# A six-layer transformer stage: q's and k's parts stored one by one and fetched in one transfer, the last head group normalised by itself, and a new written-out order

## Chip, cores and metric

The kernel runs on one core of a Trainium2 chip. The metric is the device time of one execution in microseconds (us), lower is better. TensorE (PE) does the matrix products, VectorE (DVE), ScalarE (ACT) and GpSimd (POOL) the rest, and SyncE (SP) issues every DMA of the stage that is changed.

## What is computed

The whole model adds eight blocks to a residual stream of 2 x 512 tokens of width 128. The change lies in the third, a transformer of six layers with 16 heads of width 8 and a context of 77 tokens. Its reference, cut to what matters:

```python
for i in range(NL):                                   # NL = 6
    xn = _adaln(x, noise_emb, n1_w[i], n1_b[i])       # layer norm, modulated
    q, k, v = jnp.split(xn @ qkv_w[i].T, 3, axis=-1)
    q, k = _rope(q), _rope(k)                         # B = 2, L = 512, H = 16, HD = 8
    x = x + _attn(q, k, v, src_mask).reshape(B, L, D) @ so_w[i].T
    xn = _adaln(x, noise_emb, n2_w[i], n2_b[i])
    q = _rope(xn @ cq_w[i].T); k = _rope(context @ ck_w[i].T); v = context @ cv_w[i].T
    x = x + _attn(q, k, v, ctx_mask).reshape(B, L, D) @ co_w[i].T
    xn = _adaln(x, noise_emb, n3_w[i], n3_b[i])
    x = x + gelu(xn @ f1_w[i].T + f1_b[i]) @ f2_w[i].T + f2_b[i]
```

`_attn` is a softmax over masked scores. All arithmetic is float32 in the reference.

## The kernel before

**Tiling.** A batch (one of two, `c`) has 512 tokens, four tiles of 128. Heads are taken in four groups of four (`HG` = 4). A step `a` = 2 x layer + batch is one self-attention, twelve in all; `rest(r)` is everything around it: for `r` from 2 on the cross attention and the feed-forward net that follow step `r - 2`, and for `r` below 12 the first layer norm and the q, k and v projections that precede step `r`.

**Three bfloat16 parts.** q and k are float32 values kept as three bfloat16 parts (high, middle, last). A score is a product over 48 rows of parts: six blocks of 8 rows, the block numbers of q and k paired by `Q_PARTS = (0, 0, 1, 0, 2, 1)` and `K_PARTS = (0, 1, 0, 2, 0, 1)`. The tiles `qS`, `kS` and `cS` (k of the context) hold these 48 rows, then a mask row (48) and rows for the maximum (96, 97). The projections leave q and k as 128 partitions (head x 8 + dim) x 512 tokens; the parts are made in `part3` (inside `room`) by a chain that alternates between POOL and ACT: `join` (POOL L1466), high part (ACT L1224), `rest_part` (POOL L1470), middle part (ACT L1228), `last_part` (POOL L1474). Getting them from head-major partitions into dim-major rows goes through DRAM: one store of all three parts (SP, L1549), then six transfers of 8 partitions each (`spread`, L1556), each `d h t` out of `(h d) t` in runs of 512 tokens.

**One self-attention** has two passes. The first (`maxima`, letter `m`) is 64 score products (PE L975), each reduced to a row maximum (DVE L1307) out of two PSUM banks; after each group of 16 the maxima are turned (PE L957), copied (ACT L1177) and sent into `qS` by four small DMAs (SP L1537). The second (`attend`, letter `a`) is 64 score products again (PE L1013), each with an exponential (ACT L1195), 16 times four products with V (PE L997, `weigh`), a copy of each head group's output (ACT L1186, `keep_out`), and then the normalisation: V has columns of ones, so that the outputs hold the softmax sums; POOL adds the four groups' outputs (L1447, L1443), DVE takes one reciprocal of 128 x 512 (L1321), spreads the wanted row with a shuffle per group (L1328) and multiplies groups 0 and 2 (L1333), POOL multiplies groups 1 and 3 (L1452). Then PE projects group by group (L1025, four products of 128 columns for a group, each recorded as two matmuls) and DVE adds the result to the stream `z` (L1336). The cross attention has the same scheme for all four groups: reductions L1388, reciprocal L1399, multiplications L1411 and L1506, projection L1122. The letter `r` is a piece of `rest`.

**The order of the work** on each engine is fixed by hand: each engine has generators `m`, `a` and `r`, and `weave` takes one piece of a stream per letter of the strings in `TURNS`. Before, a string has a first part, a part for a layer that is repeated, and a last part. An engine goes through its queue in order and waits at semaphores.

## Time and profile before

| | |
|---|---|
| runs | 5213.22, 5220.8, 5223.22 us, median 5220.8 |
| the profiled execution | 5205.5 us, of which its span 5203.7 |
| mean granted TensorE clock | 0.879 of 2.4 GHz over the span |
| transformer stage (2060 to 3823 us of the span) | 54 us of preparation, then 1709 us |
| busy shares over the span | PE 84%, DVE 65%, ACT 44%, POOL 10% |

Times are read from the start of the span. "Busy" counts instructions that compute; an engine's idle time before an instruction is put down to what released it. The granted clock is given as a share of full speed: 1.00 is 2.4 GHz, 0.50 is 1.2 GHz.

### The profile page before, as it was taken

How to read it: one execution, taken by the hardware profiler on the slowest of the kernel's cores; microseconds unless marked ns; L12 is line 12 of the kernel's file. 1: busy time of each engine (PE TensorE's matmuls, PEld its weight loads, DVE VectorE, ACT ScalarE, POOL GpSimd, SP SyncE). 2: the span in 40 equal slices, each digit the busy share in tenths (PEclk: the TensorE clock that was granted, in tenths of full speed). 3: DMA queues.
4: the chain of work that ended last, by engine and by line, in shares of the span. 5: the costliest groups of instructions: out<-in, count | busy, mean ns of one | idle time of the engine just before them, and what ended most of it. 6: DMA issues, size and time to landing. Idle time of an engine off the chain costs nothing. (4 is left out here: it accounts for less than half of the span.)

```text
span 5203.7 us, 88732 instructions
## 1 busy us (share of the span) xinstructions
PE 4381.7 (84%) x25098; PEld 2768.5 (53%) x25446; DVE 3406.6 (65%) x17506; ACT 2302.0 (44%) x7385; POOL 504.0 (10%) x420
## 2 busy tenths in 40 slices
PE   8999999999999987587787878778733697997979
PEld 6888888888888865223333333333322453333456
DVE  7888888888888876455555555555434594433535
ACT  4555555555555543263545454545422122332313
POOL 0000000000000001111221212222101001222000
PEclk9999999999999988697878787878765698998769
DMA  0000000000000001302222222221100010000001
GB/s 27 2 2 2 2 2 2 2 2 2 2 2 2 2 8 43 51 14 34 38 35 38 34 38 34 37 35 30 18 5 3 14 35 24 9 8 10 19 1 37
DMA packets 89492, 91.41 MB, mean 18 GB/s; under 512 B 21311, under 2 KB 84442, under 8 KB 88811
## 3 DMA queue, kind: packets, MB, share of 16 engines
q1 hardware_dynamic: 89067, 86.46, 8.6%
q8 instruction: 179, 2.93, 0.2%
q14 instruction: 246, 2.02, 0.1%
HBM read 70.22 MB, written 15.39 MB: 16 GB/s over the span
## 5 line engine op out<-in xcount | busy, mean ns | idle before, releaser
L287 DVE CUSTOM_DVE_ANT_0 I-219junk<-I-215encw,I-218expo,I-227rec 128x77 f32<-128x77 f32 x3072 | 941.1, 356 | 5.8
L1307 DVE TENSOR_REDUCE I-41381nmax<-ps 128x1 f32<-128x512 f32 x768 | 498.3, 686 | 235.7 <-PE ps L975 225.6
L1195 ACT ACTIVATE I-41384prob<-ps 128x512 f32<-128x512 f32 x768 | 428.6, 594 | 247.5 <-remote 135.4
L265 ACT ACTIVATE I-217tanh_s<-ps 128x77 f32<-128x77 f32 x1024 | 242.4, 237 | 593.9 <-PE ps L245 593.9
L245 PE MATMUL ps<-I-212hist,I-49small 128*128 128x77 f32 x2048 | 456.5, 304 | 40.6 <-DVE I-212hist L323 40.4
L245 PEld LDWEIGHTS ps<-I-212hist,I-49small 128*128 128x128 f32 x2048 | 304.9, 188 | 296.8 <-DVE I-212hist L323 296.7
L251 PE MATMUL ps<-I-217tanh_s,I-49small 128*128 128x77 f32 x2048 | 454.7, 304 | 0.0
L975 PE MATMUL ps<-I-41375kS,I-41374qS 96*128 96x512 bf16 x768 | 347.4, 479 | 111.4 <-DMA I-41374qS<-parts 53.3
L252 PE MATMUL ps<-I-212hist,I-49small 128*128 128x128 f32 x2048 | 440.0, 297 | 0.0
L247 PE MATMUL ps<-I-212hist,I-216uh_h 128*128 128x128 f32 x2048 | 439.8, 296 | 0.0
L273 ACT ACTIVATE I-223hh<-I-229gate_t,I-228pre,I-222rh 128x1 f32<-128x1 f32 x1024 | 395.5, 386 | 84.6
L248 PE MATMUL ps<-I-212hist,I-49small 128*128 128x128 f32 x2048 | 394.1, 273 | 0.0
L237 PE MATMUL ps<-I-49small 128*128 128x77 f32 x2048 | 350.9, 253 | 1.8 <-PEq L68 1.8
L323 DVE SCALAR_TENSOR_TENSOR I-212hist<-I-223hh,I-225zc,I-226zh 128x1 f32<-128x1 f32 x1024 | 224.7, 219 | 190.1 <-ACT I-223hh L273 190.1
L251 PEld LDWEIGHTS ps<-I-217tanh_s,I-49small 128*128 128x128 f32 x2048 | 304.7, 188 | 27.7
L237 PEld LDWEIGHTS ps<-I-49small 128*128 128x128 f32 x2048 | 311.1, 192 | 2.0 <-issue 2.0
L252 PEld LDWEIGHTS ps<-I-212hist,I-49small 128*128 128x128 f32 x2048 | 311.3, 192 | 0.0
L247 PEld LDWEIGHTS ps<-I-212hist,I-216uh_h 128*128 128x128 f32 x2048 | 311.2, 192 | 0.0
L248 PEld LDWEIGHTS ps<-I-212hist,I-49small 128*128 128x128 f32 x2048 | 311.0, 192 | 0.0
L1013 PE MATMUL ps<-I-41374qS,I-41375kS 128*128 128x512 bf16 x677 | 252.4, 402 | 58.0 <-ACT I-41384prob L1195 46.8
L115 POOL TENSOR_TENSOR I-59rstd<-I-58var,I-60mhalf 128x4 f32<-128x4 f32 x34 | 34.7, 1021 | 2741.9 <-DVE I-58var L99 2741.9
L257 PE MATMUL ps<-I-213zeros 128*128 128x512 bf16 x768 | 291.3, 379 | 0.0
(494 smaller groups left out, 7980.0 us busy)
## 6 DMA issues: line engine op xcount, KB each, us to landing
I-41374qS<-parts SPq DMA_DIRECT2D x144, 128.0 KB
parts<-I-41393room SPq DMA_DIRECT2D x36, 384.0 KB, 2.5
I-41375kS<-parts SPq DMA_DIRECT2D x72, 128.0 KB
I-49small<-in_layers SPq DMA_DIRECT2D x6, 768.0 KB, 19.2
I-41374qS<-I-41383mrow SPq DMA_DIRECT2D x192, 2.0 KB
I-41374qS<-I-41390crow SPq DMA_DIRECT2D x192, 2.0 KB
I-41393room<-in_own SPq DMA_DIRECT2D x5, 387.0 KB, 4.0
I-41368wk<-in_own SPq DMA_DIRECT2D x6, 320.0 KB, 12.8
```

The lines of the kernel that those rows point to most:

```text
L237: e.matmul(att[b][:, 0:S], w_e, encT[:, b * S:(b + 1) * S], start=True, stop=False)
L245: e.matmul(att[b][:, 0:S], w_h, now.to_broadcast([P, S]), start=False, stop=True).then_inc(s.att_ps, 1)
L247: e.matmul(row[:, H * wide:(H + 1) * wide], uh_h[:], now, start=True, stop=True, skip_group_check=True)
L248: e.matmul(row[:, R * wide:(R + 1) * wide], uh[:, R * P:(R + 1) * P], now, start=True, stop=True, skip_group_check=True)
L251: e.matmul(sco[b][:, 0:S], v_rep, tanh_s[:, b, :], start=True, stop=True).then_inc(s.scores, 1)
L252: e.matmul(row[:, Z * wide:(Z + 1) * wide], uh[:, Z * P:(Z + 1) * P], now, start=True, stop=True, skip_group_check=True).then_inc(s.u_ps, 1)
L257: e.matmul(k.ps[:, 7, :], zeros[:, 0:P], zeros[:], start=True, stop=True)
L273: e.activation(hh[:, b:b + 1], gate_t[:, b, R:R + 1], ACT.Tanh, scale=rh[:, b:b + 1], bias=pre[:, b, H:H + 1]).then_inc(s.hh_done, 1)
L287: return e.tensor_tensor_reduce(junk[:, 2 * g + b, :], encw[:, g, b, :], expo[:, b, :], inv[:, b:b + 1], rec[:, b, g:g + 1], ALU.mult, ALU ...
L975: e.matmul(k.ps[:, b, :], qS[0:ROWS_QK, 4 * m + j, c * T + i * P:c * T + (i + 1) * P], kS[0:ROWS_QK, 4 * m + j, c * T:(c + 1) * T], start= ...
L1195: e.activation(prob[:, tau % 2, j, :], k.ps[:, b, :], ACT.Exp, scale=scale).then_inc(free[b], 1)
L1307: e.tensor_reduce(nmax[:, U % HG, i, j:j + 1], k.ps[:, use[0], :], AX.X, ALU.max, negate=True).then_inc(free[use[0]], 1)
```

## The change

1. **Stores and spread.** The columns of the q, k, cross-q and cross-k weights are copied into dim-major order on POOL (`by_dim`, into new tiles `wk_d` and `wq_d`; `wq` is now a single buffer), so the projections leave q and k with partition dim x 16 + head. The cosine and sine tables are loaded again in that order by eight DMAs in the preparation. The DRAM tensor `parts` has six places instead of three. Each part is stored by itself as soon as it is made, into all of its places (three, two and one); one transfer then moves all 48 rows, in which the heads and tokens of a row lie one behind the other (16 KB). `qS`, `kS` and `cS` have the batch ahead of the head for that. The mask row takes four DMAs instead of two, and the memset of `cS` writes bfloat16 instead of float32.
2. **Normalisation.** POOL adds groups 0 to 2 only; DVE takes their reciprocal, and one more reciprocal for group 3 when that is there. Group 3 is multiplied on DVE instead of POOL. The same in the cross attention. Fewer columns of V are set to zero.
3. **Order.** All strings of `TURNS` are new and written out to the end, no part repeated. On SP, a layer's cross stores come ahead of the weights' loads.

```diff
-        parts_dram = nc.dram_tensor("parts", (4, 3, P, T), BF16).ap()
+        parts_dram = nc.dram_tensor("parts", (4, 6, P, T), BF16).ap()
...
+        Q_SPOTS = (slice(0, 3), slice(4, 6), slice(3, 4))
+        K_SPOTS = (slice(2, 5), slice(1, 6, 4), slice(0, 1))
...
-                    def store(name, n, m):
+                    def store(name, n, m, which, spots):
                         spot = SPOT[name]
-                        e.wait_ge(s.last, job[r, name])
-                        if times(r, name) > 1:
-                            e.wait_ge(jsent[spot], 96 * (times(r, name) - 1))
-                        e.dma_start(parts_dram[spot, :, :, 0:m].rearrange("r p t -> p r t"),
-                                    part3[:, n, :, 0:m]).then_inc(jstored[spot], 16)
-
-                    def spread(name, m, dst, order):
+                        e.wait_ge((s.jhigh, s.middle, s.last)[which], job[r, name])
+                        if which == 0 and times(r, name) > 1:
+                            e.wait_ge(jsent[spot], 16 * (times(r, name) - 1))
+                        dst = parts_dram[spot, spots, :, 0:m].rearrange("r p t -> p r t")
+                        e.dma_start(dst, part3[:, n, which, 0:m].unsqueeze(1).to_broadcast(dst.shape)).then_inc(jstored[spot], 16)
+
+                    def spread(name, m, dst):
                         spot = SPOT[name]
-                        e.wait_ge(jstored[spot], 16 * times(r, name))
-                        for row, which in enumerate(order):
-                            e.dma_start(dst[8 * row:8 * row + 8, :, c * m:(c + 1) * m],
-                                        parts_dram[spot, which, :, 0:m].rearrange("(h d) t -> d h t", d=8)).then_inc(jsent[spot], 16)
+                        e.wait_ge(jstored[spot], 48 * times(r, name))
+                        e.dma_start(dst[0:ROW_MASK, c, :, :],
+                                    parts_dram[spot, :, :, 0:m].rearrange("r (d h) t -> (r d) h t", h=NH)).then_inc(jsent[spot], 16)
+
+                    def deliver(name, n, m, dst, places):
+                        for which, spots in enumerate(places):
+                            store(name, n, m, which, spots)
+                            yield
+                        spread(name, m, dst)
+                        yield
...
+                    def by_dim(dst, src, ready):
+                        e.tensor_copy(dst[:, 0:512].rearrange("p (n d h) -> p n d h", n=4, d=8),
+                                      src[:, 0:512].rearrange("p (n h d) -> p n d h", n=4, d=8)).then_inc(ready, 1)
...
-                    e.wait_ge(s.pooled, 3 * (a + 1))
-                    e.reciprocal(inv[:], inv[:]).then_inc(s.inv, 1)
-                    yield
                     for n in range(HG):
                         U = HG * a + n
-                        e.wait_ge(s.inv, a + 1)
+                        if n == 0:
+                            e.wait_ge(s.pooled, 2 * (a + 1))
+                            e.reciprocal(inv[:], inv[:]).then_inc(s.inv, 1)
+                            yield
+                        if n == HG - 1:
+                            e.wait_ge(*done(values(a, n)))
+                            e.wait_ge(s.wide, U)
+                            e.reciprocal(inv[:], o[:, n, :]).then_inc(s.inv, 1)
+                        e.wait_ge(s.inv, 2 * a + 1 + n // (HG - 1))
                         if U >= 2:
                             e.wait_ge(s.normed, U - 1)
                         e.stream_shuffle(wide[:, n % 2, :], inv[:], [8 + n] * 32).then_inc(s.wide, 1)
-                        if n % 2 == 0:
+                        if n != 1:
```

Written out by name from the strings, this is PE's queue around the end of step 5 (S: scores of the second pass, W: `weigh`, O: output projection of a group, M: maxima of step 6, R6 and R7: pieces of `rest`; "ln2" the turn of a layer norm, "qx" q's projection, "kx" the context's k, "cv" the context's values, "sx", "tx", "txs" projections of k and q, "v" of the values):

```text
before  S5.14.0-1 W13 R6.txs R6.v0 S5.14.2-3 S5.15.0 R6.v1 R6.v2 S5.15.1 W14 S5.15.2-3 R6.v3 R7.kx W15 O0 O1 O2 O3 R7.ln2 R7.qx R7.cv M6.0.0 ...
after   R6.txs ... R6.v3 R7.kx S5.12.0 ... S5.14.2-3 S5.15.0-1 W14 S5.15.2-3 W15 O0 O1 O2 O3 M6.0.0-3 R7.ln2 M6.0.4-5 R7.qx R7.cv M6.0.6 ...
```

At the very start PE's queue before has the projections of `R0` and `R1` (16 pieces) and then the maxima of step 0; after it has those of `R0` (8 pieces), then 29 pieces of step 0's maxima and their turn up to M0.1.4 with the two passes and `R1` mixed from there on. Around step 2, txs of `R2` is 10 pieces ahead of M2.0.0 before and 31 pieces after. DVE's queue around the end of step 5 is, before, `R6.tturn recip N0 N1 N2 N3 add R7.ln2`, and after the same names in the same order, with the second reciprocal inside N3; in the cross attention of `R6` it is, after, `M5.2.7 recip N0 N1 M5.2.8 N2 N3 M5.2.9`.

## Rows read from the trace of the kernel before

**Rows 1.** Windows by stage: time, busy of each engine (instructions), clock, DMA share, GB/s

```profile
2060.00:2114.00 54.00, 15.52 (x72) 15.43 (x72) 25.29 (x12) 0.14 (x1) 19.12 (x27) 0.50 0.17 51
2114.00:3823.00 1709.00, 1322.44 (x6509) 534.73 (x6600) 925.29 (x1908) 815.38 (x1560) 328.48 (x300) 0.81 0.20 33
```

**Rows 2.** Groups by line, 2060 to 3900 us: busy, mean ns, idle before, releasers

```profile
L1307 DVE TENSOR_REDUCE I-41381nmax<-ps 128x1 f32<-128x512 f32 x768 | 498.3, 686 | 235.7 <-PE ps L975 225.6
...
L975 PE MATMUL ps<-I-41375kS,I-41374qS 96*128 96x512 bf16 x768 | 347.4, 479 | 111.4 <-DMA I-41374qS<-parts 53.3 <-DVE I-41381nmax L1307 43.0 <-ACT I-41383mrow L1177 0.2
L1013 PE MATMUL ps<-I-41374qS,I-41375kS 128*128 128x512 bf16 x677 | 252.4, 402 | 58.0 <-ACT I-41384prob L1195 46.8 <-issue 5.2
...
L1025 PE MATMUL ps<-I-41369wso,I-41385o 128*128 128x128 f32 x384 | 73.9, 370 | 72.6 <-DVE I-41385o L1333 72.5
...
L1086 PE MATMUL ps<-I-41376cS,I-41374qS 96*128 96x77 bf16 x768 | 61.0, 236 | 32.8 <-DMA I-41374qS<-parts 30.1 <-issue 0.7 <-DVE I-41388cmax L1388 0.2
...
L1321 DVE RECIPROCAL I-41387inv<-I-41387inv 128x512 f32<-128x512 f32 x12 | 40.2, 3353 | 154.5 <-POOL I-41387inv L1443 154.5
L1399 DVE RECIPROCAL I-41392cinv<-I-41392cinv 128x512 f32<-128x512 f32 x12 | 40.2, 3350 | 39.5 <-POOL I-41392cinv L1496 39.5
```

**Rows 3.** PE in order of time: start, us [idle before and its releaser]

```profile
2162.07 1.03 PE L975 MATMUL ps<-I-41375kS,I-41374qS 96*128 96x512 bf16 x2 [12.97 <-DMA I-41374qS<-parts]
...
2395.78 1.03 PE L975 MATMUL ps<-I-41375kS,I-41374qS 96*128 96x512 bf16 x2 [19.12 <-DMA I-41374qS<-parts]
...
2788.13 5.42 PE L1025 MATMUL ps<-I-41369wso,I-41385o 128*128 128x128 f32 x24 [7.09 <-DVE I-41385o L1333]
...
3722.38 2.84 PE L1025 MATMUL ps<-I-41369wso,I-41385o 128*128 128x128 f32 x24
...
3794.54 6.57 PE L1122 MATMUL ps<-I-49small,I-41393room 128*128 128x128 f32 x32 [7.06 <-DVE I-41393room L1411]
```

**Rows 4.** ACT and DVE in order of time: the work between the two

```profile
2781.11 0.60 ACT L1186 ACTIVATE I-41385o<-ps 128x512 f32<-128x512 f32 x1 [1.19 <-PE ps L997]
...
2786.47 0.72 DVE L1328 STREAM_SHUFFLE I-41386wide<-I-41387inv 128x512 f32<-128x512 f32 x1
2787.29 0.69 DVE L1333 TENSOR_TENSOR I-41385o<-I-41385o,I-41386wide 128x512 f32<-128x512 f32 x1
```

**Rows 5.** Windows around one such wait, columns as in rows 1

```profile
2784.00:2786.00 2.00, 0.00 (x0) 0.00 (x0) 2.00 (x1) 0.00 (x0) 0.00 (x0) 0.50 1.03 141
...
2812.00:2822.00 10.00, 8.36 (x18) 1.94 (x19) 8.65 (x15) 1.57 (x3) 1.15 (x1) 0.50 0.21 56
2840.00:2848.00 8.00, 7.33 (x64) 2.86 (x63) 6.03 (x16) 6.28 (x14) 0.00 (x0) 1.00 0.02 5
```

**Rows 6.** The way of the last cross q through DRAM, in order of time

```profile
3742.43 1.15 POOL L1474 TENSOR_TENSOR I-41393room<-I-41393room 128x512 bf16<-128x512 f32 x1 [0.74 <-ACT I-41393room L1228]
3743.61 0.38 SPq L1549 DMA_DIRECT2D parts<-I-41393room  x1
3746.16 2.10 SPq L1556 DMA_DIRECT2D I-41374qS<-parts  x6
...
3759.40 2.23 PE L1086 MATMUL ps<-I-41376cS,I-41374qS 96*128 96x77 bf16 x24 [21.84 <-DMA I-41374qS<-parts]
```

**Rows 7.** Windows with a spread alone, and with the first loads of the program

```profile
3746.00:3758.00 12.00, 0.00 (x0) 0.00 (x0) 0.00 (x0) 0.00 (x0) 0.00 (x0) 0.50 0.49 65
...
4.00:6.00 2.00, 0.00 (x0) 0.00 (x0) 0.00 (x0) 0.00 (x0) 0.00 (x0) 1.00 1.08 430
```

**Rows 8.** POOL's end of q's parts for step 0

```profile
2132.75 1.15 POOL L1474 TENSOR_TENSOR I-41393room<-I-41393room 128x512 bf16<-128x512 f32 x1 [0.74 <-ACT I-41393room L1228]
```

**Rows 9.** The preparation, DVE and SP in order of time

```profile
2068.68 1.08 DVE L882 MEMSET I-41376cS<- 128x1232 f32 x1 [0.20 <-issue]
...
2087.41 2.11 DVE L885 MEMSET I-41376cS<- 2x2464 bf16 x1 [0.46 <-issue]
...
2091.03 0.58 SPq L845 DMA_DIRECT2D I-41376cS<-I-41393room  x1
```

More of the change, by code:

```diff
@@ L786, in rest_order, with transformer @@
     return out
-def transformer(nc, k, small, z, ctxT, own_dram, layers, masks, rows, sel_dram):
+def transformer(nc, k, small, z, ctxT, own_dram, layers, masks, rows, small_dram):
     with ExitStack() as ctx:
@@ L843, in _ @@
                 e.wait_ge(s.filled, 4)
-                for dst, row in ((kS, maskrow[:, 0:B * T]), (cS, maskrow[:, B * T:B * (T + S)])):
-                    e.dma_start(dst[ROW_MASK:ROW_MASK + 1, :, :],
-                                row.unsqueeze(1).to_broadcast([1, NH, row.shape[1]])).then_inc(s.sent, 16)
-                e.wait_ge(s.sent, 16 * 2)
+                for c in range(B):
+                    for dst, at, m in ((kS, c * T, T), (cS, B * T + c * S, S)):
+                        e.dma_start(dst[ROW_MASK:ROW_MASK + 1, c, :, :],
+                                    maskrow[:, at:at + m].unsqueeze(1).to_broadcast([1, NH, m])).then_inc(s.sent, 16)
+                e.wait_ge(s.sent, 16 * 2 * B)
                 e.dma_start(mods[0], own_dram[0][:, 0:774]).then_inc(s.mods, 16)
-                e.wait_ge(s.own, 16 * 2)
+                at = offsets(SMALL)[0]["cos"][0]
+                for d in range(8):
+                    e.dma_start(small[16 * d:16 * d + 16, at:at + 2 * T], small_dram[d:P:8, at:at + 2 * T]).then_inc(s.own, 16)
+                e.wait_ge(s.own, 16 * 10)
             @block.gpsimd
@@ L858, in _ @@
                     for g in range(HG):
-                        for n in range(HG):
-                            if n != g:
+                        for n in range(HG - 1):
+                            if n != g and g < HG - 1:
                                 e.memset(dst[:, :, 4 * g:4 * g + 4, 8 + n:9 + n], 0.0).then_inc(s.ones, 1)
@@ L983, in attend @@
                     l, c = divmod(a, B)
-                    tok = slice(c * T, (c + 1) * T)
                     def weigh(t):
@@ L1162, in rest @@
                             b = open_bank(e, use)
-                            e.matmul(k.ps[:, b, 0:P], mine[:, i * P:(i + 1) * P], K(4), start=True, stop=True).then_inc(full[b], 1)
+                            e.matmul(k.ps[:, b, 0:P], mine[:, i * P:(i + 1) * P], wk[:, 512:640], start=True, stop=True).then_inc(full[b], 1)
                             yield
@@ L1222, in high_part @@
                             last = jobs[job[r, name] - 3]
-                            e.wait_ge(jstored[SPOT[last[1]]], 16 * times(*last))
+                            e.wait_ge(jstored[SPOT[last[1]]], 48 * times(*last))
                         e.activation(part3[:, n, 0, 0:m], flat[:, n, 0:m], ACT.Copy).then_inc(s.jhigh, 1)
@@ L1597, in rest @@
                     if r < NA:
-                        store("k", 0, T)
-                        yield
-                        store("q", 1, T)
-                        yield
-                        spread("k", T, kS, K_PARTS)
-                        yield
-                        spread("q", T, qS, Q_PARTS)
-                        yield
+                        yield from deliver("k", 0, T, kS, K_SPOTS)
+                        yield from deliver("q", 1, T, qS, Q_SPOTS)
                 weave(TURNS["sync"], m=all_of(maxima), r=all_rest(rest))
@@ L2343, in model @@
         layer_norm(nc, k, x, nT, keep=z)
-        transformer(nc, k, small, z, g_("ctxT"), A["own"], A["layers"], (A["mask1"], A["mask2"]), A["l1f2b"], A["sel"])
+        transformer(nc, k, small, z, g_("ctxT"), A["own"], A["layers"], (A["mask1"], A["mask2"]), A["l1f2b"], A["small"])
         add_stream(nc, x, z)
```

250 lines of the change are left out of this document (145 added, 105 removed).

## The prediction

> **What bounds the kernel now.** I read the windows by stage first. The transformer stage takes 54 us of preparation and 1709 us of work; in the latter PE is busy 1322 us (77%), DVE 925 (54%), ACT 815, POOL 328, at a mean granted clock of 0.81 [rows 1]. So PE's queue is the longest, and 387 us of it are gaps. The groups by line name them [rows 2]: PE stands 72.5 us at the output projection (L1025) for the normalised groups, 53.3 us at the first maxima (L975) and 30.1 us at the first cross maxima (L1086) for a DMA of parts, 46.8 us at the scores for an exponential, 43.0 us at the maxima for DVE's reductions. In order of time these are few and long: 12.97 us ahead of step 0, 19.12 us ahead of step 2, 7.09 us at the end of a step, 7.06 us in the last cross attention [rows 3]; at the very end 21.84 us for the last cross q [rows 6]. The remaining waits for parts, 53.3 - 12.97 - 19.12 = 21.2 us in nine and 30.1 - 21.84 = 8.3 us in four, are 2 us each. Since PE stands there with nothing else to do, a us taken from such a wait is a us of the kernel, as long as no other wait takes its place.
>
> **The way through DRAM.** The last cross q shows it alone [rows 6]: the last part is done at 3743.6, the store is issued at once, the spread at 3746.16 (2.55 us later) and PE starts at 3759.4, 13.2 us after that. The six transfers move 786 KB at 65 GB/s with 0.49 to 0.57 of 16 engines busy, which is 12 us [rows 7]. That is eight partitions at a time in runs of 1 KB. The same queue moved the program's first loads, 128 partitions with long rows, at 430 GB/s [rows 7]. The new spread has 48 partitions and rows of 16 KB. Its moving time lies between 786 KB / 430 = 1.8 us and the old 12 us; I take 4, nearer the fast end since both the run length and the number of partitions go the way of that row, plus the 2 us that a small transfer needs here anyway (2.55 for the store): 6 us from issue to landing for 13.2. The store of the last part alone has a third of the bytes, and the others are issued under POOL's and ACT's chain: 2.2 us for 2.55. One trip falls from 15.8 to 8.2 us; bounds 6 and 16.
>
> The Trainium skill (DMA: Bandwidth & Descriptors, "Why a DMA increments its semaphore by 16 and not by 1") says that a transfer is split over the largest number of engines up to 16 that divides the slowest dimension of both sides: eight for the old transfers, sixteen for the new, and the half-busy engines agree with that. Its page SBUF — State Buffer ("Door 1") puts partitions 0 to 47 on 8 of 16 ports of 435 GB/s together; by that the new spread moves at 218 GB/s at most, 3.6 us.
>
> **The terms**, summed against the profiled execution's own 5205.5 us.
>
> *Start, -18.* q's parts of step 0 are ready at 2133.9 [rows 8], but PE starts its maxima only at 2162.1 [rows 3]: k's and q's spreads share the queue, then weights and the next batch's stores come in. With 8.2 us and k's ahead of it, 2144 is due after the preparation is 2.3 us later: the memset of `cS` in bfloat16 costs 2.11 for 1.08 by the row of the same number of columns, and two more mask DMAs at 0.6 us each lie on SP ahead of the modulation's load [rows 9]. By that step 0 starts 18 us earlier. R1's pieces now lie between its maxima; PE is paced by DVE's 0.62 us there and has room, and the second pass starts 8 maxima sooner, so I set these against each other. Bounds -8 and -25. The reload of the sine tables (8 DMAs) and the first POOL copy lie under the modulation's matmuls and under DVE's first norm; uncovered they'd cost about 3 and 1.3 us.
>
> *Step 2, -17.* PE's 19.12 us [rows 3] end with q's landing. Before, q's last projection (txs) is 10 pieces ahead of the maxima, now 31; PE's queue has 2616 pieces, 0.65 us each over 1709 us [rows 1], so 20 us instead of 6.5. The parts take 6 us from the projection (3737.6, where PE's 21.84 us begin, to 3743.6 [rows 6]), k's begin about 2 us ahead of q's, and two spreads of 4 us follow: 6 + 2 + 8 + 2 = 18 at most. About 2 stay.
>
> *End of a step, -49.* Between PE's last weighing (2781.0) and its next matmul lie the copy of group 3 (0.60), POOL's sum, the reciprocal (3.35), a shuffle (0.72) and a multiplication (0.69): 7.09 us [rows 2 to 4]. Groups 0 to 2 no longer wait: group 2 is complete sixteen exponentials earlier, and DVE is idle there (154.5 us of idleness ahead of L1321 in 12 steps [rows 2]). Group 3 needs 0.60 + 3.35 + 0.72 + 0.69 and some 0.35 of hand-overs, 5.7 us, during which PE projects three groups, 2.84 us at full clock [rows 3], up to 3.7. What stays is 2.0 to 2.9; I take 2.4 of a mean 6.6 in eleven places: -46, and -3 for the twelfth and for POOL's multiplications, which are off the way. What is queued behind DVE's new wait in N3 is only the addition to z, which waits for PE anyway.
>
> *Small waits for parts, -20.* Nine and four waits, 29.5 us in all, with 7 us taken from each trip; a third is kept, since 18 us against 20 is a narrow margin at each step.
>
> *The clock, -20.* After the 7 us wait the granted clock is 0.50, still 0.50 from 2812 to 2822, and 1.00 from 2840 on [rows 5]. The first 24 matmuls of L1025 took 5.42 us there and 2.84 at 3722, where no long wait came first [rows 3]: 2.6 us, and about 1 more for the projections behind it; the DVE-paced maxima lose nothing. 3.6 x 10 = 36; the shorter waits still lower it at times, so I take about half. Bounds 0 and -36.
>
> *The end, -12.* 7.6 from the last trip and 4.6 from the last cross projection's 7.06.
>
> *Costs, +10.* DVE gets 24 reciprocals and 24 multiplications more, 24 x (3.35 + 0.69) = 97 us. The twelve of the self-attention fall into its idleness. The twelve of the cross attention are among the maxima, with only 39.5 us idle ahead of the old one [rows 2]; PE's next maxima must wait out 3.35 us or find other work. Bounds 0 and +40; a quarter, since PE's order has scores and weighings there. POOL's 13 copies of 128 x 512 (about 1.2 us, as its other operations of that size [rows 6]) replace 24 additions and fall between norms, where it is idle; uncovered 16 us. Zeroed columns are fewer. The smaller number of issues on SP (4 for 7) is worth nothing to PE.
>
> *The order, -10.* 90 us of PE's waits (exponentials and reductions, [rows 2]) can be moved only by the order of the queues, for either sign. R6's projections leave the last quarter of a step, which ACT paces, for its middle. Bounds -40 and +25.
>
> Sum: -18 - 17 - 49 - 20 - 20 - 12 + 10 - 10 = -136. The profiled execution would be 5069.5; against the median of the runs, which lies 15 us above it, 5085.
>
> **The rivals.**
> *The spread is only half as fast* (12%), 8 us of moving for 4. For it: each old transfer, too, filled single partitions, and 16 engines at the old 8 GB/s each (65 over 8) give 6. Then k's and q's last landing is 26 us behind txs for PE's 20: 6 us at each of ten steps instead of the third kept, start -12, end -8, half the clock: 5130.
> *DVE becomes the limit* (12%). If the 97 us delay the reductions by 55 beyond my 10, 5140. For it: PE already waits 43.0 us for reductions and is paced by them in the first groups of a step; against it: DVE 54% busy, becoming 60%.
> *The order recovers more* (20%): the clock stays up and the waits for exponentials shrink, 6 us for each of ten steps, 5025.
> *Slower* (5%): the spread stays at 65 GB/s. For it: one transfer is issued where six were, and if it is not split over more engines, nothing makes it faster. k and q then move for 24 us in a row, and q lands 6 + 2 + 24 + 2 = 34 us behind txs where PE arrives after 20; some of that PE's order absorbs at a lower pace, I take 11 left at each of ten steps. Start -4, step 2 -10, step ends -49, waits for parts +85, end -5, clock 0, costs +10, order -10: +17, 5238. It decides from a moving time of about 11 us on; with four engines it would be +200 and more. Against it: the row of 430 GB/s, and loads later in the program whose DRAM side is one contiguous piece.
> *No change* (2%): new waits cancel the gain.
>
> **How the numbers follow.** 49% for the forecast (5060 to 5115), 12, 12, 20, 5 and 2% for the others. 5020 to 5160 holds the forecast, both weak gains and half of the strong one: a little over 8 in 10. Within 0.2% (10 us, what a measurement of this kernel can tell) lies 3%; slower 5%; faster 92%.
>
> **What would show it.** The wait at L1025 for DVE: 20 to 30 us in all instead of 72.5, now at the fourth group. L975 and L1086 for parts under 20 together, for 83. Spread from issue to PE's start about 6 us at the end, windows above 150 GB/s. First maxima at 2144. Mean clock of the stage 0.85 or more. Idle PE for reductions above 60 us would show DVE's rival. The prediction is wrong if the steps, 133.5 us apart between 2788 and 3722 (seven steps, [rows 3]), stay above 130, whatever the start gives.

## The result and the profile after

The changed kernel takes 5090.43 us (median of 5089.45, 5089.49, 5091.37 and 5112.34), the one before 5219.66 (four runs, 5213.22 to 5223.22): a ratio of 0.9764, 95% interval 0.9736 to 0.9792. The forecast was 5085. The profiled execution is the one of 5112.34 us; its transformer stage ends (L121) at 3709.9 against 3829.9, 119.9 us earlier. Behind the stage the two kernels are the same, and there this execution lost 27 us again. The windows of the last stretch show that, first of after, then of before (columns as in rows 1):

```profile
4500.00:5110.00 610.00, 537.30 (x2198) 304.95 (x2196) 248.05 (x547) 164.60 (x290) 48.28 (x24) 0.79 0.05 15
```

```profile
4620.00:5203.00 583.00, 511.19 (x2196) 290.27 (x2195) 248.28 (x547) 164.01 (x289) 48.26 (x24) 0.83 0.05 16
```

The same matmuls (2198 and 2196 records) take 26 us more of PE at a granted clock of 0.79 instead of 0.83. The other three runs of after are some 22 us shorter, at a mean clock of 0.889 to 0.891 for 0.886; where in them the time was saved no trace shows. Such swings are in several kernels here (one gave 5067.5 to 5112.3 us, with a mean clock of 0.894 to 0.884), so below I read small effects at the end of the transformer stage, and whole kernels by ratios.

The windows by stage, of after [compare rows 1]; as there, the second window ends 6.9 us before the stage's end:

```profile
2060.00:2116.00 56.00, 15.52 (x72) 15.44 (x72) 26.32 (x12) 0.00 (x0) 18.16 (x15) 0.50 0.19 59
2116.00:3703.00 1587.00, 1284.00 (x6600) 526.10 (x6600) 1018.67 (x1956) 817.26 (x1560) 282.81 (x270) 0.84 0.20 45
```

The work is 122 us shorter than in [rows 1]; PE is busy 81% of it, DVE 64%, the clock is 0.84 for 0.81. (Before, 91 of PE's records are missing, all at L1013, so that some 30 us of its busy time there may stand as idle.) The groups by line, 2060 to 3731 us [compare rows 2]:

```profile
L1005 PE MATMUL ps<-I-41377kS,I-41376qS 96*128 96x512 bf16 x768 | 331.5, 460 | 131.2 <-DVE I-41383nmax L1336 67.7 <-DMA I-41376qS<-parts 50.8 <-ACT I-55xh L1239 2.9
L1042 PE MATMUL ps<-I-41376qS,I-41377kS 128*128 128x512 bf16 x768 | 281.1, 408 | 53.2 <-ACT I-41386prob L1224 45.1 <-DMA I-41376qS<-I-41385mrow 3.6
...
L1115 PE MATMUL ps<-I-41378cS,I-41376qS 96*128 96x77 bf16 x768 | 67.1, 247 | 16.7 <-DMA I-41376qS<-parts 15.6 <-DVE I-41390cmax L1422 0.3
...
L1054 PE MATMUL ps<-I-41369wso,I-41387o 128*128 128x128 f32 x384 | 50.3, 283 | 24.6 <-DVE I-41387o L1367 21.1 <-issue 3.5
...
L1358 DVE RECIPROCAL I-41389inv<-I-41387o 128x512 f32<-128x512 f32 x12 | 40.2, 3353 | 28.3 <-ACT I-41387o L1215 28.3
```

The wait of the output projection (now L1054) has gone from 72.5 to 21.1 us. The wait for parts at the first maxima has gone only from 53.3 to 50.8, and that at the cross maxima from 30.1 to 15.6, all in the last one. The wait for reductions has grown from 43.0 to 67.7, but the matmuls at the same line are busy 331.5 us for 347.4. Each is awaited by a reduction of 0.69 us on DVE, out of two banks, so what PE saves there comes back as waiting. Busy time and this wait together are 399.2 us for 390.4, 8.8 more. PE in order of time shows one end of a step, and behind it the next step's wait for q:

```profile
2352.04 2.92 PE L1054 MATMUL ps<-I-41369wso,I-41387o 128*128 128x128 f32 x24 [0.16 <-issue]
2356.94 1.16 PE L1054 MATMUL ps<-I-41369wso,I-41387o 128*128 128x128 f32 x8 [1.98 <-DVE I-41387o L1367]
2361.64 1.03 PE L1005 MATMUL ps<-I-41377kS,I-41376qS 96*128 96x512 bf16 x2 [3.54 <-DMA I-41376qS<-parts]
```

Three groups are projected in 2.92 us where they took 5.42 [rows 3]: no 7 us wait comes first, and the granted clock is 1.00 from 2352 to 2355, for 0.57 from 2788 to 2794 before. The fourth follows after 1.98 us. SP and PE at the start of step 0:

```profile
2128.92 3.91 SPq L1608 DMA_DIRECT2D parts<-I-41395room  x3
2134.22 0.33 SPq L1613 DMA_DIRECT2D I-41377kS<-parts  x1
2134.59 1.85 SPq L1608 DMA_DIRECT2D parts<-I-41395room  x3
2144.08 0.32 SPq L1613 DMA_DIRECT2D I-41376qS<-parts  x1
```

```profile
2151.87 1.03 PE L1005 MATMUL ps<-I-41377kS,I-41376qS 96*128 96x512 bf16 x2 [19.15 <-DMA I-41376qS<-parts]
```

q's stores are issued by 2136.4, but its spread, which waits for their landing, only at 2144.1. k's spread, issued ahead of them at 2134.2, landed 8.0 us later, so the stores landed only after it. The page's list of DMA issues gives the spreads' landing (median us from issue, the last number):

```profile
I-41376qS<-parts SPq DMA_DIRECT2D x24, 768.0 KB, 7.7
...
I-41377kS<-parts SPq DMA_DIRECT2D x12, 768.0 KB, 8.1
```

### The profile page after: what moved, and what is told of

Its sections match the earlier page's. It is cut to its first block and busy times, and to the rows that moved or that the text cites. A ratio compares the mean times of both kernels' runs of the same rounds, so it can differ in the third digit from the quotient of the medians.

```text
span 5110.6 us, 88969 instructions
## 1 busy us (share of the span) xinstructions
PE 4407.6 (86%) x25446; PEld 2771.9 (54%) x25446; DVE 3501.4 (69%) x17554; ACT 2304.4 (45%) x7385; POOL 457.8 (9%) x378
## 5 line engine op out<-in xcount | busy, mean ns | idle before, releaser
L1336 DVE TENSOR_REDUCE I-41383nmax<-ps 128x1 f32<-128x512 f32 x768 | 499.1, 686 | 215.0 <-PE ps L1005 208.1
L1224 ACT ACTIVATE I-41386prob<-ps 128x512 f32<-128x512 f32 x768 | 427.8, 595 | 199.0 <-PE ps L1042 196.3
L1005 PE MATMUL ps<-I-41377kS,I-41376qS 96*128 96x512 bf16 x768 | 331.5, 460 | 131.2 <-DVE I-41383nmax L1336 67.7
L257 PE MATMUL ps<-I-213zeros 128*128 128x512 bf16 x1024 | 388.3, 379 | 0.0
L1042 PE MATMUL ps<-I-41376qS,I-41377kS 128*128 128x512 bf16 x768 | 281.1, 408 | 53.2 <-ACT I-41386prob L1224 45.1
```

Source lines behind the costliest of these rows:

```text
L257: e.matmul(k.ps[:, 7, :], zeros[:, 0:P], zeros[:], start=True, stop=True)
L1005: e.matmul(k.ps[:, b, :], qS[0:ROWS_QK, c, 4 * m + j, i * P:(i + 1) * P], kS[0:ROWS_QK, c, 4 * m + j, :], start=True, stop=True, skip_grou ...
L1224: e.activation(prob[:, tau % 2, j, :], k.ps[:, b, :], ACT.Exp, scale=scale).then_inc(free[b], 1)
L1336: e.tensor_reduce(nmax[:, U % HG, i, j:j + 1], k.ps[:, use[0], :], AX.X, ALU.max, negate=True).then_inc(free[use[0]], 1)
```

## The experiments

Ratios are to the kernel before, measured on the same chip beside each run. The first group takes the change apart into its three parts, with all combinations. Where a part brings pieces of its own, each queue has them at their place in the kernel that they come from, moved only where an engine would otherwise wait for itself. Two changes of SyncE's order come with the stores and not with the order: the cross stores ahead of the weights' loads, and k's spread ahead of q's stores (before, k's and q's stores were issued first and then both spreads).

**Normalisation alone.** The queues, stores and spreads of before.

```diff
-                    e.wait_ge(s.pooled, 3 * (a + 1))
...
+                        if n == HG - 1:
+                            e.wait_ge(*done(values(a, n)))
...
+                            e.reciprocal(inv[:], o[:, n, :]).then_inc(s.inv, 1)
```

> The kernel before with only the new normalisation (three groups summed, a second reciprocal for the fourth); transfers and the order of the pieces stay old. My terms: the waits for the normalised groups fall from 72.5 us to about 25, the clock gives some 15 us, the second reciprocals cost 10: about 5170 us. Rival, the gain of the change lies in the order: under 15 us here, above 5205. Rival, DVE becomes the limit: the waits for reductions grow by more than 20 us from 43, about 5195.

Measured: 1.0083 (1.0056 to 1.0110), median 5260.8 us: longer by 0.8%, little but clear of the noise, where 5170 was expected. PE's groups:

```profile
L931 PE MATMUL ps<-I-41375kS,I-41374qS 96*128 96x512 bf16 x768 | 350.8, 484 | 192.9 <-DMA I-41374qS<-parts 119.2 <-DVE I-41381nmax L1263 59.3 <-ACT I-41383mrow L1133 0.2
...
L981 PE MATMUL ps<-I-41369wso,I-41385o 128*128 128x128 f32 x384 | 59.4, 317 | 30.1 <-DVE I-41385o L1294 23.3 <-issue 6.9
```

The wait for the groups fell as it should, 72.5 to 23.3, and the wait for parts behind it grew from 53.3 to 119.2: PE arrives earlier at maxima whose q isn't there. The cost on DVE shows too: busy time and the wait for reductions at this line make 410.1 us together, 19.7 more than before.

**Stores and spread alone.** The weights' columns, the six places, the single spread; the normalisation and order of before.

```diff
-        parts_dram = nc.dram_tensor("parts", (4, 3, P, T), BF16).ap()
+        parts_dram = nc.dram_tensor("parts", (4, 6, P, T), BF16).ap()
...
+                        e.dma_start(dst[0:ROW_MASK, c, :, :],
+                                    parts_dram[spot, :, :, 0:m].rearrange("r (d h) t -> (r d) h t", h=NH)).then_inc(jsent[spot], 16)
```

> The kernel before with only the new stores and the one spread (and the copies of the weights that it needs); normalisation and the order of PE, DVE and ACT stay old. My terms: first maxima 10 us earlier, the 19 us ahead of step 2 down to 5, the last cross q 6 us earlier, the small waits for parts gone (29 us to 5): about 5165 us. Rival, the old order hides the trips anyway and only the three long waits shrink: about 5190. Rival, the trip is no shorter where two spreads follow each other: above 5205.

Measured: 0.9931 (0.9908 to 0.9954), median 5174.0 us, near the 5165 expected. The wait for parts at the first maxima falls from 53.3 to 7.5 us, that of the projection stays at 72.5, and the wait for ACT's normalised `xh` (L1042 of before) grows from 43.1 to 62.6.

**Order alone.** The strings of PE and ACT as in the changed kernel; those of DVE, POOL and SP differ by the pieces that the old work has more or at another place. The work of before.

```diff
-    tensor=("rrrrrrrrrrrrrrrrmmmmmmmmmmrmmmmmmmmmmmmmmmmmmmmmmmmmaamamammamaammaamamaammaamamaammaammmmmmmaamammaamammaamma"
...
+    tensor=("rrrrrrrrmmmmmmmmmmmmmmmmmmmmmmrmmrmmaarmmaamamaammaarmaamramaammamarrammaamamaammaarmammaammaarmamaamaammamama
...
```

> The new order of the pieces on all engines with the old six-transfer spread and the old normalisation; POOL's and DVE's pieces of the normalisation are moved behind q's last part where the new order would lock them. My reading: the new order leaves 20 us between q's projection and the maxima, the old trip of k and q needs over 30, so a wait of about 10 us stands at most steps: 5230 to 5300 us. Rival, the order is what brings the gain: 5130 to 5180.

Measured: 1.0353 (1.0321 to 1.0385), median 5397.9 us, above the 5230 to 5300 expected. PE waits 141.1 us for parts at the first maxima and 95.1 at the cross maxima, and 47.7 at the cross attention's projection for DVE's normalised groups.

**The three pairs**: the edits above, two at a time.

```diff
+ stores and spread (second edit)   + normalisation (first edit)
+ stores and spread (second edit)   + order (third edit)
+ normalisation (first edit)        + order (third edit)
```

> Both parts of the change in the old order. My terms: the two gains add but for a little, about 5120 us; what the new order brings is then the rest to 5090. Rival, the order carries most: above 5150.

> The changed kernel with the old normalisation (its pieces on POOL and DVE moved behind q's last part where the new order would lock them). The 7 us wait at the end of a step comes back in eleven places, with the low clock behind it: 50 to 75 us above the changed kernel, 5140 to 5165. Rival, the second reciprocals cost about what they bring: within 15 us of 5090.

> The changed kernel with the old store of all parts and six transfers per spread. The trips of k and q then need over 30 us where the order gives them 20: waits for parts of about 10 us at each step, 100 us above the changed kernel, about 5190 to 5230. Rival, the spread is hidden anyway but for start and end: 5110 to 5120.

Expected were 5120, 5140 to 5165 and 5190 to 5230 us; the medians are 5139.4, 5241.7 and 5340.3. The first lies between the two theories, the other two are far above both: where the new order is without one of its partners, it costs much more than I had expected.

| parts of the change | ratio (interval) | waits of PE for q's and k's parts (first maxima) | for the normalised groups | busy at the first maxima + wait for reductions | end of the stage |
|---|---|---|---|---|---|
| none | 1 | 53.3 us | 72.5 | 390.4 | 3829.9 |
| normalisation | 1.0083 (1.0056 to 1.0110) | 119.2 | 23.3 | 410.1 | 3863.7 |
| stores | 0.9931 (0.9908 to 0.9954) | 7.5 | 72.5 | 390.4 | 3785.1 |
| order | 1.0353 (1.0321 to 1.0385) | 141.1 | 81.0 | 390.7 | 4015.7 |
| stores, normalisation | 0.9856 (0.9830 to 0.9882) | 7.3 | 29.6 | 410.8 | 3760.9 |
| stores, order | 1.0043 (1.0026 to 1.0059) | 19.2 | 81.0 | 397.4 | 3852.3 |
| normalisation, order | 1.0235 (1.0218 to 1.0252) | 205.8 | 21.1 | 390.3 | 3942.1 |
| all three | 0.9764 (0.9736 to 0.9792) | 50.8 | 21.1 | 399.2 | 3709.9 |

The faster spread is worth 0.7% alone, 2.3% with the new normalisation, 3.1% with the new order and 4.7% with both. The normalisation costs 0.8% alone; with the new spread it gains 0.75%, with the new order 1.2%, with both 2.8%. The new order costs 3.5% alone and 1.1 and 1.5% with one other part; it gains 0.9% only on top of both. No part can be priced by itself.

A part of what the normalisation gains under the new order lies in the cross attention, for which the table has no column. With the old normalisation PE waits there for DVE's groups (stores and order):

```profile
L1086 PE MATMUL ps<-I-49small,I-41395room 128*128 128x128 f32 x384 | 66.1, 332 | 49.6 <-DVE I-41395room L1375 49.6
```

It is 7.5 us before and 5.9 in the changed kernel. In the two runs of the new order without the new normalisation, pieces of the old one had to be moved, so this wait may be due to where they were put; another place was not tried.

**Spreads by themselves.** Ahead of the kernel, transfers of 786 KB from DRAM, one kind after the other, each awaited before the next; a second round repeated them. `(h d)` and `(h q)` give runs of 1 KB, `(d h)` and `(q h)` rows that lie in one piece.

```diff
+                for rep in range(2):
+                    for r in range(6):
+                        go(e.dma_start(t[8 * r:8 * r + 8, :, :], d[P * r:P * r + P].rearrange("(h d) t -> d h t", d=8)))
+                    land()
+                    for r in range(6):
+                        go(e.dma_start(t[8 * r:8 * r + 8, :, :], d[P * r:P * r + P].rearrange("(d h) t -> d h t", d=8)))
+                    land()
+                    go(e.dma_start(t[0:48, :, :], d.rearrange("(h q) t -> q h t", q=48)))
+                    land()
+                    go(e.dma_start(t[0:48, :, :], d.rearrange("(q h) t -> q h t", q=48)))
+                    land()
+                    go(e.dma_start(t[40:88, :, :], d.rearrange("(q h) t -> q h t", q=48)))
+                    land()
+                    go(e.dma_start(t[0:96, 0:8, :], d.rearrange("(q h) t -> q h t", q=96)))
+                    land()
+                    go(e.dma_start(t[:, 0:6, :], d.rearrange("(q h) t -> q h t", q=P)))
+                    land()
```

> The changed kernel with a stage ahead of everything that times 786 KB transfers one by one out of DRAM: six of 8 partitions in runs of 1 KB, the same in rows of 16 KB, one of 48 partitions in runs of 1 KB, one in rows of 16 KB, the latter also at partitions 40 to 87, one of 96 and one of 128 partitions. If the number of engines and ports decides: six transfers of 8 about 14 us from issue to landing with either run length, 48 partitions about 7 with either, partitions 40 to 87 below that, 128 about 4. If the run length decides: 16 KB rows are faster in both forms, 1 KB runs slow in both. The time of the kernel is longer by the stage.

Measured (SP in order of time; the time to the next line is one transfer with its landing, the last line begins the second round):

```profile
20.39 2.12 SPq L2371 DMA_DIRECT2D I-101probe_tile<-probe_dram  x6
33.77 1.96 SPq L2374 DMA_DIRECT2D I-101probe_tile<-probe_dram  x6
47.45 0.32 SPq L2376 DMA_DIRECT2D I-101probe_tile<-probe_dram  x1
55.10 0.31 SPq L2378 DMA_DIRECT2D I-101probe_tile<-probe_dram  x1
62.86 0.30 SPq L2380 DMA_DIRECT2D I-101probe_tile<-probe_dram  x1
68.46 0.30 SPq L2382 DMA_DIRECT2D I-101probe_tile<-probe_dram  x1
73.85 0.34 SPq L2384 DMA_DIRECT2D I-101probe_tile<-probe_dram  x1
78.00 2.10 SPq L2371 DMA_DIRECT2D I-101probe_tile<-probe_dram  x6
```

Six transfers of 8 partitions take 13.4 and 13.7 us, one of 48 partitions 7.65 and 7.76, with runs of 1 KB and rows of 16 KB alike (7.47 and 7.80 in the second round); the run length makes no difference that shows. The partitions do: 5.6 us for 48 of them at 40 to 87, 5.4 for 96, 4.15 for 128. As "partitions 0 to 47" and "40 to 87" move the same rows of the same DRAM tensor, it is the place in SBUF that takes the 2.2 us.

The Trainium skill (SBUF — State Buffer, "Door 1: The DMA port swizzle") lists which partitions share one of 16 ports. By its table partitions 0 to 47 put eight on the fullest port and 40 to 87 at most four. An estimate from its 435 GB/s for 16 ports: 8 x 16 KB through one port is 4.8 us, 4 x 16 KB 2.4 us. The measured 7.8 and 5.6 us differ by 2.2, so the trace agrees. By the same estimate 96 partitions take 2.4 us and 128 take 1.8; the measured 5.4 fits that, 4.15 is lower than it says. The prediction's 3.6 us shared the bytes evenly over the eight ports of partitions 0 to 47.

**The rows at partitions 40 to 87**, in the changed kernel:

```diff
-ROW_MASK = 48
+ROW_FIRST = 40
+ROW_MASK = 88
...
-                        e.dma_start(dst[0:ROW_MASK, c, :, :],
+                        e.dma_start(dst[ROW_FIRST:ROW_MASK, c, :, :],
```

> The changed kernel with q's, k's and the context's 48 rows of parts held at partitions 40 to 87 in place of 0 to 47 (the mask's row at 88, zeros below), nothing else. Theory (what is left of the waits for parts is the landing of the spread, and the landing is set by which partitions it writes: 5.6 us for 7.8 in the run of spreads by themselves): the median landing of q's and k's spread falls by about 2 us each, the waits for parts (67.7 us of 12 maxima, 15.6 at the last cross maxima) fall by 20 to 45 us, the first maxima begin 2 to 4 us earlier, and the time falls by 10 to 30 us, to 5060 to 5080. Rival (the landing is set by something else in the kernel, such as the other transfers beside it or the wait of the stores behind k's spread, and the maxima wait anyway for DVE and ACT): landings within 0.5 us of before, time 5085 to 5095.

Measured: 0.9762 (0.9729 to 0.9795), median 5083.4 us. The landings and PE's first maxima:

```profile
I-41376qS<-parts SPq DMA_DIRECT2D x24, 768.0 KB, 6.0
...
I-41377kS<-parts SPq DMA_DIRECT2D x12, 768.0 KB, 6.1
...
L1006 PE MATMUL ps<-I-41377kS,I-41376qS 96*128 96x512 bf16 x768 | 331.7, 460 | 112.9 <-DVE I-41383nmax L1337 67.1 <-DMA I-41376qS<-parts 31.5 <-ACT I-55xh L1240 2.9
```

Both landings are 1.7 and 2.0 us shorter, the wait is 31.5 us for 50.8, step 0 starts at 2148.15, 3.7 us earlier, and the stage ends at 3697.4 for 3709.9. (The 67.7 us that the expectation names is the wait for reductions; that for parts was 50.8.) The mechanism is as the theory has it, and it is worth 12.6 us in the profiled stage. The waits for parts fell by 21.1 us in all; 6.2 of that came back as a longer wait for `xh` (28.9 us for 22.7). In the whole kernel's time, 0.9762 for 0.9764, a gain of this size is within the interval and does not show.

**The fourth group in halves**, in the changed kernel:

```diff
-                            e.reciprocal(inv[:], o[:, n, :]).then_inc(s.inv, 1)
+                            h = slice(0, T // 2)
+                            e.reciprocal(inv[:, h], o[:, n, h]).then_inc(s.inv_h, 1)
...
+                            e.tensor_tensor(o[:, n, h], o[:, n, h], wide[:, n % 2, h], ALU.mult).then_inc(s.normed_h, 1)
+                            h = slice(T // 2, T)
...
```

> The changed kernel with self-attention's fourth group made in two halves of 256 columns (reciprocal, shuffle and multiplication of columns 0 to 255, then those of 256 to 511), and PE's projection of the first two token tiles waiting for the first half alone. Theory (PE's eleven waits of about 2 us for the fourth group are on the path that sets the end): the waits for o fall from 21.1 us to under 5, DVE is busy about 0.2 us longer in each step, the time falls by 10 to 20 us, to 5070 to 5080. Rival (DVE has become a limit of the step beside PE, so that what PE doesn't wait for here it waits for at the next maxima, nmax or xs): the waits for o fall as much, the waits for DVE elsewhere grow by as much, time 5085 to 5100.

Measured: 0.9784 (0.9762 to 0.9806), the stage's end at 3712.1, 2.1 us later. Both theories missed the wait itself:

```profile
L1056 PE MATMUL ps<-I-41369wso,I-41387o 128*128 128x128 f32 x384 | 51.2, 285 | 23.7 <-DVE I-41387o L1373 20.3 <-issue 3.5
...
L1361 DVE RECIPROCAL I-41389inv<-I-41387o 128x256 f32<-128x256 f32 x12 | 21.0, 1752 | 27.4 <-ACT I-41387o L1217 27.4
...
L1364 DVE STREAM_SHUFFLE I-41388wide<-I-41389inv 128x256 f32<-128x256 f32 x12 | 5.3, 438 | 0.0
...
L1367 DVE TENSOR_TENSOR I-41387o<-I-41387o,I-41388wide 128x256 f32<-128x256 f32 x12 | 5.1, 425 | 1.2
```

Two halves take 2 x (1.75 + 0.44 + 0.43) = 5.24 us for 3.35 + 0.73 + 0.73 = 4.81, and PE has only 0.6 us of work on the first half to hide under the second. It now waits as long for the second one, 20.3 us.

**q's stores ahead of k's spread**, in the changed kernel (the order in which the kernel before had them):

```diff
-                        yield from deliver("k", 0, T, kS, K_SPOTS)
-                        yield from deliver("q", 1, T, qS, Q_SPOTS)
+                        for which, spots in enumerate(K_SPOTS):
+                            store("k", 0, T, which, spots)
+                            yield
+                        for which, spots in enumerate(Q_SPOTS):
+                            store("q", 1, T, which, spots)
+                            yield
+                        spread("k", T, kS)
+                        yield
+                        spread("q", T, qS)
+                        yield
```

> The changed kernel with SyncE's order changed at the end of each self-attention's row: k's three stores, q's three stores, k's spread, q's spread, in place of k's stores and spread, then q's. The same transfers. Theory (q's stores stand behind k's spread of 8 us in the DMA queues, and q's landing, the one that the maxima wait for, is late by that): q's spread is issued 3 to 6 us earlier at the first maxima, the first maxima begin 2 to 5 us earlier, the waits for parts fall by 10 to 30 us, the time by 5 to 25 us. Rival (q's parts are made so much later than k's in the later steps that k's spread, held back for them, becomes the late one, and the two spreads share the same ports in turn): q's landing does not come earlier in the later steps, waits for parts the same or up to 20 us more, time 5085 to 5110.

Measured: 0.9823 (0.9797 to 0.9849), the stage's end at 3734.5, 24.6 us later: the rival, a little beyond its bounds (waits for parts 24.1 us more, median 5110.9). SP at step 0 and around 2350 us, and PE's group:

```profile
2136.42 0.43 SPq L1613 DMA_DIRECT2D I-41377kS<-parts  x1
2137.77 0.31 SPq L1613 DMA_DIRECT2D I-41376qS<-parts  x1
...
2351.22 0.43 SPq L1613 DMA_DIRECT2D I-41377kS<-parts  x1
2352.57 0.32 SPq L1613 DMA_DIRECT2D I-41376qS<-parts  x1
...
L1005 PE MATMUL ps<-I-41377kS,I-41376qS 96*128 96x512 bf16 x768 | 329.8, 457 | 156.8 <-DMA I-41376qS<-parts 74.9 <-DVE I-41383nmax L1336 66.9 <-ACT I-55xh L1239 2.9
```

q's spread goes out 6.3 us earlier at step 0, yet the maxima start at 2150.59, 1.3 us earlier: the two spreads move side by side, and 14.2 us pass from the first issue to the maxima (12.8 from the second) where one spread takes 7.7. So in this run the moving time of the two spreads sets the start, and not the place of q's stores. Later k's spread is held back for q (issued at 2351.2, for 2344.2), and PE waits 8.5 us for 3.5.

**All three of these edits together** (their diffs as above).

> The changed kernel with all three edits: rows of parts at partitions 40 to 87, the fourth group in halves, q's stores ahead of k's spread. If each was worth what its theory says and they act on different waits (those for parts, and that for the fourth group), the time falls by the sum, 30 to 60 us, to 5030 to 5060. If DVE and ACT have become the limits of a step, it falls by no more than the best one of them alone, and PE's waits for nmax, xs and free score banks take the rest: 5060 to 5095.

Measured: 0.9769 (0.9744 to 0.9793), the stage's end at 3694.3, 3.1 us ahead of the best of them alone; 38.4 us of waits for parts. The three stage gains, 12.6, -2.1 and -24.6, would add up to 14.1 us later; together they are 15.6 earlier. They don't add up.

**Without the second reciprocal** of self-attention:

```diff
-                            e.reciprocal(inv[:], o[:, n, :]).then_inc(s.inv, 1)
...
-                        e.stream_shuffle(wide[:, n % 2, :], inv[:], [8 + n] * 32).then_inc(s.wide, 1)
+                        e.stream_shuffle(wide[:, n % 2, :], inv[:] if n < HG - 1 else o[:, n, :], [8 + n] * 32).then_inc(s.wide, 1)
```

> The changed kernel without the second reciprocal of self-attention (left out: the fourth group is multiplied by its own sums and not by their reciprocals; shuffle and multiplication stay). It prices what the changed kernel pays on DVE for having the fourth group apart: 12 reciprocals of 3.35 us, 40.2 us of DVE. Theory after the split in halves (PE's waits for the fourth group, 21.1 us, are all that is left of it on the path, since the rest lies beside PE's maxima and projections): the waits for o go, those for nmax fall by under 10 us, the Transformer's end comes 20 to 30 us earlier than 3709.9, the time is 5060 to 5075. Rival (DVE is what bounds a step, so that all of its 40 us comes back): the waits for nmax fall by 15 to 30 us as well, the end comes 35 to 50 us earlier, the time is 5040 to 5060. Second rival (parts, maxima's banks and ACT take up what DVE gives, as they did when the stores were reordered): under 15 us earlier, 5080 to 5095.

Measured: 0.9764 (0.9739 to 0.9789), the stage's end at 3703.2, 6.8 us earlier: the second rival.

```profile
L1005 PE MATMUL ps<-I-41377kS,I-41376qS 96*128 96x512 bf16 x768 | 330.6, 458 | 148.1 <-DMA I-41376qS<-parts 67.6 <-DVE I-41383nmax L1336 67.6 <-ACT I-55xh L1239 3.2
...
L1054 PE MATMUL ps<-I-41369wso,I-41387o 128*128 128x128 f32 x384 | 46.6, 277 | 3.5 <-issue 3.5
```

The 21.1 us of waits for the fourth group are gone, and 16.8 us of them reappear one line further on, as a longer wait for q. DVE has 40.2 us less to do and PE's wait for reductions stays at 67.6: DVE's second reciprocals in the self-attention cost PE nothing there.

## Why the prediction came out right, and where its steps did not

The forecast of the whole was right within 0.1%, by its likeliest case. The steps, 133.5 us apart before, are now 125.8 (the first group's projections at 2728.10 and 3608.67, seven steps), under the 130 that the forecast named as its limit. Of its other signs the waits at L1025 came in (21.1 us); the mean clock of the stage (0.84 for 0.85), the first maxima, the last spread from its issue to PE's start (7.8 us for about 6), the waits for parts and those for reductions did not. The terms stand so:

- **End of a step, -49: right.** 72.5 us became 21.1, a gain of 51.4, with 1.98 us left at most steps for the 2.4 forecast. *The clock, -20: right.* L1054 is busy 50.3 us for 73.9, 23.6 less. L1005 is 15.9 less busy as well, but there DVE sets the pace, as the prediction says, and the time went into waiting. Over all its lines PE is busy 38 us less.
- **Start, -18: mis-sized.** The preparation was longer as forecast (the wait for the modulation 40.6 us for 38.7), but step 0 starts at 2151.9, 10.2 us earlier, and not at 2144. The step that failed is "I take 4" for the moving time, with 6 us from issue to landing: it is 7.7 and 8.1, midway between the forecast and the rival of a spread half as fast. (That rival's 5130 does not come out of its own terms, which add up to about 5153.) In the run of spreads by themselves the row length, one of my two reasons for a value near the fast end, changes nothing. q's spread had to wait for k's on top; the run with q's stores first gained 1.3 us there. The 10.2 us are not all gain: PE's wait ahead of step 0 is 19.15 us for 12.97, since R1's projections no longer fill it.
- **Step 2, -17, and small waits for parts, -20: mis-sized.** The 19.12 us wait is gone, but nine waits for parts are left at the first maxima, 50.8 us. Without step 0's they are 31.7, where I kept a third of the small ones. "L975 and L1086 for parts under 20 together" came out as 66.4; the sign was too low by the prediction's own terms too, which leave 14.2 at the last cross q, 9.8 of the small ones and 2 at step 2, without step 0's. The failed step is "The parts take 6 us from the projection", which I read from the last cross q, when ACT had nothing else to do. In a step ACT's queue holds exponentials, in order of time (POOL, ACT, POOL, ahead of the 3.54 us wait above):

```profile
2342.21 1.16 POOL L1509 TENSOR_TENSOR I-41395room<-I-41395room 128x512 f32<-128x512 f32 x1 [0.22 <-ACT I-41395room L1253]
```

```profile
2350.36 0.65 ACT L1257 ACTIVATE I-41395room<-I-41395room 128x512 bf16<-128x512 f32 x1
```

```profile
2351.09 1.16 POOL L1513 TENSOR_TENSOR I-41395room<-I-41395room 128x512 bf16<-128x512 f32 x1 [3.26 <-ACT I-41395room L1257]
```

q's remainder is ready at 2343.4, and ACT makes the middle part of it 7 us later, behind the exponentials; spread at 2353.99, maxima at 2361.64. It is so at all seven steps where PE waits 3.5 us or more for q: the middle part is made 6.0 to 7.0 us after its input is ready. So in the changed kernel it is this way, and not the fourth group, that sets when such a step begins. Two runs agree: taking 2 us from the landing gave 12.6 us, 3.7 of them at the start; taking the 2 us of the group's wait away gave 6.8. Moving the middle part ahead in ACT's queue was not tried. In the old order of the queues the same spreads leave 7.5 us of these waits, and 7.3 with the new normalisation.
- **The end, -12: 9.1.** From the last part (3632.75) to PE's start (3642.28) it is 9.5 us for 15.8, where 8.2 was forecast, and 2.8 us come from there to the stage's end. The spread was issued 1.7 us after the last part and moves at 164 GB/s in its best window of 2 us, as "above 150" had it (119 and 115 in the windows beside it):

```profile
3636.00:3638.00 2.00, 0.00 (x0) 0.00 (x0) 0.00 (x0) 0.00 (x0) 0.00 (x0) 0.50 1.03 164
```

- **Costs, +10: right, but its sign misled.** Waits for reductions grew by 24.7, to 67.7, above the 60 that I named for DVE's rival. 15.9 of that is what the shorter matmuls of L1005 saved; busy time and wait together grew by 8.8. That one turns into the other shows in four kernels of the table: the matmuls are busy 347.4, 339.9, 333.3 and 330.8 us, and the sum stays at 390.3 to 390.7. DVE's rival is not borne out: the sum is 390.3 us for 390.7 with and without the new normalisation under the new order and the old stores, 399.2 for 397.4 with the new stores, and 398.2 without the second reciprocals of the self-attention. Only in the old order does the new normalisation cost what I feared, 19.7 and 20.4 us. Why the new order and the new stores together have 6.7 us more than the new order alone stays open.
- **The order, -10: the sign right, the manner not.** I treated it as an item that adds up. On top of both other parts it is worth 0.9%, without them it costs 3.5%. What it brings in the changed kernel is mostly PE's wait for ACT's normalised `xh` (L1070, L1042 before), 22.7 us for 43.1: with the order alone it is 21.8, in the old order with the new stores and normalisation 62.1. The prediction looked for it in the waits for exponentials, which stayed (45.1 for 46.8). The comparison of 20 us of PE's work for 18 us of transfer was the right kind of argument; it should have been made for each part with the others absent.

Added up, the rows give start -10, end of a step -51, waits for parts in the later steps and the cross maxima -17 (31.7 us for the 40.3 of [rows 3] and their nine small ones, and none for 8.3), the end -9, maxima +9, clock -24, `xh` -20: -122 beside the stage's -120. It is a sum of the large items only: by all of its rows PE is 38 us less busy and 82 us less idle in the stage, 17 of the latter in small waits that no term names, and the start's 10 us are in part R1's projections, moved behind it. Gains that I had set too high by 8, 20 and 3 us were made up by waits for `xh` that brought 10 more than the whole term of the order, and by 7 us in the clock, the step's end and the costs. So the total was right partly by luck. The slower rival, the old moving time under the new order, was run too: normalisation and order without the spread gave 1.0235 where I had 5238 us, 1.0033. Its mechanism was real: the waits for parts went to 205.8 us at the first maxima and 93.1 at the cross maxima, 215 more than before, where I had +85. I had let PE's order absorb far too much of it.

## What to carry to other kernels

When a wait on the busiest engine is removed, look at the next thing that it will wait for, and price that with the engine arriving earlier: twice here (normalisation alone, no second reciprocal) most of the gain, or more than all of it, reappeared as a wait for q's transfer. Where another engine paces a stretch, read the busy time and the wait together: a longer wait there can be nothing but shorter matmuls. A chain that alternates between engines must be timed where their queues are full, not at the quiet end of the program. Splitting a producer in halves gains only what the consumer can do on the first half, less the fixed cost of each half.

## What was unexpected of the hardware

A transfer of 786 KB into 48 partitions takes 7.5 to 7.8 us whether its runs are 1 KB or 16 KB, and 5.6 us when the same 48 rows lie at partitions 40 to 87 instead of 0 to 47. Two spreads issued 1.35 us apart took 14.2 us from the first issue to the matmul that waited for both, little less than one behind the other. Halving the columns of a reciprocal (512 to 256) takes it from 3.35 to 1.75 us, a shuffle from 0.73 to 0.44, so most of their time is by the column.
